# A selective scan and a mixture of experts on one core: the order of TensorE's slot, the last chain, the ring of gate rows and the adder of every fourth state

## The reference, cut to what matters

```python
x = x + mamba_block(ln_c(x))         # x: (4, 128, 16, 16); 4 batches, 128 channels, 256 positions
# inside: four chunks of 32 channels, each: h = dA * h + (dt*x) * B_t for 16 states, 256 steps,
#         y = sum over states of h * C_t; y = (y + xc * D) * silu(z); out projection; layer norm; proj
t = to_tokens(x)
t = t + moe(ln_t(t))                 # 16 experts, hidden 256, top 2 by router logits
#         out = sum over e of ce[e] * ((silu(t @ wg[e]) * (t @ wu[e])) @ wd[e]), all experts computed
```

## Time and profile before

| | us |
|---|---|
| median of 3 runs (lowest, highest) | 334.9 (333.28, 337.46) |
| the profiled execution's own time | 334.86 |
| its span, first to last instruction | 333.1 |
| mean granted TensorE clock, share of full | 0.969 |
| PE busy | 290.8 |
| DVE busy | 238.1 |
| POOL busy | 168.4 |
| ACT busy | 152.4 |

### The profile page before, as it was taken

The page is one execution under the profiler, slowest core; times in us unless marked ns, Lnnn a source line. Parts: engine busy times, 40 slices in busy tenths (PEclk is TensorE's granted clock), DMA queues, the critical chain, the costliest instruction groups (busy, mean ns, idle before and its releaser), DMA issues.

```text
span 333.1 us, 3808 instructions
## 1 busy us (share of the span) xinstructions
PE 290.8 (87%) x1172; PEld 212.2 (64%) x1172; DVE 238.1 (71%) x380; ACT 152.4 (46%) x228; POOL 168.4 (51%) x155
## 2 busy tenths in 40 slices
PE   7986799989699989876699887688899998699996
PEld 5842645545355767654576766466678786588885
DVE  2479899999586976989769769877864364355543
ACT  2578755535453337564333376533423562222221
POOL 5000898886338566877498659765821220322310
PEclk9999769999979999999979999979999999999999
DMA  7991666337822864655748666641110200221110
GB/s 262 349 281 39 201 211 201 126 126 202 191 85 78 200 186 129 186 143 135 212 107 224 173 145 171 157 130 64 47 37 28 63 31 4 63 80 48 48 32 16
DMA packets 21748, 43.39 MB, mean 130 GB/s; under 512 B 2848, under 2 KB 8032, under 8 KB 21728
## 3 DMA queue, kind: packets, MB, share of 16 engines
q1 hardware_dynamic: 16848, 34.09, 36.1%
q10 hardware_dynamic: 4880, 9.07, 9.5%
HBM read 42.03 MB, written 1.11 MB: 130 GB/s over the span
## 4 chain that ended last, share of the span: by engine, by line
PE 44%; issue 28%; POOL 14%; DVE 8%; ACT 4%; DMA 1%; POOLq 0%; DVEq 0%; ACTq 0%
PE bank L730 17%; POOL y L311 7%; PE bank L911 7%; PE bank L878 7%; PE bank L896 7%; POOL u L304 5%; PE bank L734 3%; DVE y L567 2%; POOL xs L318 2%; DMA X<-x 1%; ACT th L500 1%; PE bank L792 1%; ACT bank L438 1%; DVE dt L571 1%; DVE y L576 1%
## 5 line engine op out<-in xcount | busy, mean ns | idle before, releaser
L500 ACT ACTIVATE th<-bank,cst 128x512 f32<-128x512 f32 x64 | 44.0, 687 | 131.6 <-PE bank L878 131.5
L304 POOL TENSOR_TENSOR u<-dtx,BCs 128x512 f32<-128x512 f32 x64 | 81.0, 1276 | 15.3 <-DVE h L624 14.6
L896 PE MATMUL bank<-xs,Wu 128*128 128x256 f32 x256 | 67.9, 388 | 21.6 <-DVE hid L694 15.1
L686 DVE SCALAR_TENSOR_TENSOR th<-th,bank 128x512 f32<-128x512 f32 x64 | 43.9, 686 | 59.4 <-ACT th L500 59.2
L318 POOL TENSOR_TENSOR xs<-xm,Gs 128x512 f32<-128x512 f32 x32 | 41.0, 1283 | 83.5 <-DMA Gs<-CE_far 79.3
L896 PEld LDWEIGHTS bank<-xs,Wu 128*128 128x128 f32 x256 | 47.5, 192 | 37.9 <-issue 20.8
L878 PE MATMUL bank<-xm,Wg 128*128 128x256 f32 x256 | 67.5, 387 | 0.0
L911 PE MATMUL bank<-hid,Wd 128*128 128x256 f32 x256 | 67.0, 386 | 0.0
L438 ACT ACTIVATE bank<-dt,cst,A 128x510 f32<-128x510 f32 x64 | 49.6, 775 | 20.1 <-DVE h L624 17.8
L878 PEld LDWEIGHTS bank<-xm,Wg 128*128 128x128 f32 x256 | 49.8, 195 | 7.5 <-issue 0.5
L911 PEld LDWEIGHTS bank<-hid,Wd 128*128 128x128 f32 x256 | 48.5, 192 | 8.5 <-issue 2.1
(11 more groups left out here) (120 smaller groups left out, 220.1 us busy)
## 6 DMA issues: line engine op xcount, KB each, us to landing
BCs<-BC_far SPq DMA_DIRECT2D x72, 256.0 KB, 4.1
Gs<-CE_far ACTq DMA_DIRECT2D x32, 256.0 KB, 3.4
BCs<-BC_far SPq DMA_DIRECT2D x56, 128.0 KB, 3.1
Wg<-gate_w SPq DMA_DIRECT2D x1, 2048.0 KB, 10.7
Wu<-up_w SPq DMA_DIRECT2D x1, 2048.0 KB, 16.2
par<-params ACTq DMA_DIRECT2D x1, 597.5 KB, 4.4
X<-x SPq DMA_DIRECT2D x2, 256.0 KB, 4.7
BC_far<-BC_rows SPq DMA_DIRECT2D x4, 128.0 KB, 3.0
```

The lines of the kernel that those rows point to most:

```text
L304: g.tensor_tensor(u[:, k % U_RING], dtx[:, k // NS, :], BCs[:, k % BC_RING, 0], ALU.mult)\
L500: a.activation(th[:, n % 2], bank[gate_bank(n)][:], ACT.Tanh, scale=0.5, bias=zero).then_inc(S["th_r"], 1)
L686: v.scalar_tensor_tensor(th[:, n % 2], th[:, n % 2], 1.0, bank[gate_bank(n)][:], ALU.add, ALU.mult)\
L896: o = t.matmul(bank[up_bank(n)][:, f * T:(f + 1) * T], Wu[:, e, f * P:(f + 1) * P], xs[:, pr % 2, ts], start=True, stop=True)
```

## The change

G_RING goes from 3 to 4, and ACT issues each spread one pair of items further ahead (three of them where a batch begins). PE's slot becomes `gate(n+1)`, `up(n)`, chain item, `down(n-2)`, `sum_state`; `gate(0)` goes before the last of the first 28 steps and waits for weighed state 25 of those instead of 26 (bank 2's last reader is step 24). States 3, 7, 11 of the last two batches (k % 4 == 3) are summed by PE instead of POOL, for which the product with D, which starts the bank's sum, moves from offset 11 to 3. The last batch's chain has a table of its own, `BESIDE_TAIL`, in which the later items come 1 to 2 offsets earlier and ACT's "spread" is at offset 9. The warming products go from 8 to 11 at the start and from 16 to 4 before the projections, and end two steps earlier in the steps; the products of the variance go ahead of those that prepare weights.

```diff
--- before.py
+++ after.py
@@ -38,7 +38,7 @@
 LAG = 2
 BY_PE = 2 * NS
 BC_RING = 6
-G_RING = 3
+G_RING = 4
 U_RING = HC_RING = 4
 H_RING = 3
 LAST_C2 = FIRST - 2
@@ -48,9 +48,11 @@
                 "PE": {1: "out", 2: "var", 4: "centre", 5: "var_t", 7: "logits", 8: "turn", 9: "x1"},
                 "ACT": {1: "sq", 2: "rstd", 4: "sq_t", 5: "rstd_t", 7: "exp", 8: "gates", 9: "x1", 10: "spread"}}
 BESIDE_ITEMS = {"DVE": {0: "gated", 3: "norm", 6: "tokens", 7: "top", 8: "mix"},
-                "PE": {0: "total", 1: "out", 2: "var", 4: "centre", 5: "var_t", 7: "logits", 9: "turn", 10: "x1",
-                       11: "skip_D"},
+                "PE": {0: "total", 1: "out", 2: "var", 4: "centre", 5: "var_t", 7: "logits", 9: "turn", 10: "x1", 3: "skip_D"},
                 "ACT": {1: "sq", 2: "rstd", 4: "sq_t", 5: "rstd_t", 8: "exp", 9: "gates", 10: "x1"}}
+BESIDE_TAIL = {"DVE": {0: "gated", 2: "norm", 4: "tokens", 5: "top", 6: "mix"},
+               "PE": {0: "total", 1: "out", 2: "var", 3: "centre", 4: "var_t", 5: "logits", 7: "turn", 8: "x1"},
+               "ACT": {1: "sq", 2: "rstd", 3: "sq_t", 4: "rstd_t", 6: "exp", 7: "gates", 8: "x1", 9: "spread"}}
 
 F32, F32R, U32 = mybir.dt.float32, mybir.dt.float32r, mybir.dt.uint32
 ALU, ACT = mybir.AluOpType, mybir.ActivationFunctionType
@@ -183,7 +185,7 @@
 
 
         def by_pe(k):
-            return k < BY_PE or k % NS == NS - 1
+            return k < BY_PE or k % 4 == 3
 
         def red_count(k):
             return sum(1 for i in range(k) if by_pe(i))
@@ -202,7 +204,7 @@
             b, o = divmod(k, NS)
             if b - 1 not in range(BATCH):
                 return None, None
-            table = (BESIDE_STEPS if b == 1 else BESIDE_ITEMS)[engine]
+            table = (BESIDE_STEPS if b == 1 else BESIDE_TAIL if b == BATCH else BESIDE_ITEMS)[engine]
             return table.get(o), b - 1
 
         block = ctx.enter_context(nc.Block())
@@ -490,8 +492,10 @@
                     act.wait_ge(S["bias_r"], 1)
                     a.activation(X[:, b, :], bank[R][:, T:2 * T], ACT.Identity, bias=bias[:]).then_inc(S["x1_r"], 1)
                 if item == "spread":
-                    spread_gate(0)
-                    spread_gate(1)
+                    spread_gate(b * E // 2)
+                    spread_gate(b * E // 2 + 1)
+                    if b == 0:
+                        spread_gate(2)
 
             def gate_tanh(n):
                 act.wait_ge(S["g_r"], n + 1)
@@ -519,10 +523,11 @@
                 if k + 1 < STEPS:
                     decay(k + 1)
                 back(*chain("ACT", k), True)
-                if n % E == E - 2 and n + 2 < ITEMS:
+                if n % E == E - 2 and n // E < BATCH - 2:
                     spread_gate(n // 2 + 1)
-                pr = n // 2 + 2
-                if n % 2 == 0 and pr < ITEMS // 2 and 2 * pr % E:
+                    spread_gate(n // 2 + 2)
+                pr = n // 2 + 3
+                if n % 2 == 0 and pr < ITEMS // 2 and pr % (E // 2) > 1:
                     spread_gate(pr)
 
         @block.vector
@@ -734,25 +739,25 @@
                     t.matmul(bank[b][:, 0:P], mean_w[:], mean_w[:], start=True, stop=True)
 
             pe.wait_ge(S["mean_c"], 1)
-            keep_warm(8, 6)
+            keep_warm(11, 6)
             pe.wait_ge(S["M_r"], 1)
             for i in range(2):
                 pe.wait_ge(S[f"x_in{i}"], 16)
                 mm(bank[i][:], M[:], half(X, i), "cen_r")
+            pe.wait_ge(S["const0"], 7)
+            for i in range(2):
+                pe.wait_ge(S["sq_r"], i + 1)
+                mm(bank[2 + i][:], var_in_w, half(sq, i), "var_r")
             pe.wait_ge(S["par_in"], 16)
             mm(bank[7][:, 0:P], p("out0"), M[:], "prep_r")
             mm(bank[7][:, P:2 * P], p("out1"), M[:], "prep_r")
             mm(bank[7][:, 2 * P:3 * P], p("dt_in"), p("dt_out"), "prep_r")
             mm(bank[7][:, 3 * P:3 * P + 1], p("proj"), p("norm_b"), "prep_r")
             mm(bank[6][:, 0:P], p("proj_t"), M[:], "prep_r")
-            pe.wait_ge(S["const0"], 7)
-            for i in range(2):
-                pe.wait_ge(S["sq_r"], i + 1)
-                mm(bank[2 + i][:], var_in_w, half(sq, i), "var_r")
             pe.wait_ge(S["bias_r"], 1)
             pe.wait_ge(S["projw_r"], 2)
             mm(bank[6][:, P:P + 1], M[:], bias[:], "bias_p")
-            keep_warm(16, 5)
+            keep_warm(4, 5)
 
             def project_in(i, base, weights, name):
                 for turn, (b, q) in enumerate(((0, 0), (1, 1), (0, 1), (1, 0))):
@@ -852,15 +857,6 @@
                     t.matmul(r2, proj_w[:], chk[:, b, :], start=True, stop=False)
                     mm(r2, ident[:], X[:, b, :], "x1p_r", False, True)
 
-            for k in range(FIRST):
-                back(*chain("PE", k))
-                if k + 1 < FIRST:
-                    spread_c(k + 1)
-                if k:
-                    sum_state(k - 1)
-                if k < FIRST - 2:
-                    keep_warm(1, 7)
-
             def gate(n):
                 b, e = divmod(n, E)
                 if n == 0:
@@ -871,7 +867,7 @@
                 if j:
                     pe.wait_ge(S["m_r"], j)
                 elif n == 0:
-                    pe.wait_ge(S["hc_r"], LAST_C2)
+                    pe.wait_ge(S["hc_r"], LAST_C2 - 1)
                 else:
                     pe.wait_ge(S["scan_r"], FIRST)
                 for f in range(FH):
@@ -912,16 +908,25 @@
                                  start=e == 0 and f == 0, stop=e == E - 1 and f == FH - 1)
                 o.then_inc(S["yd_r"], 1)
 
-            gate(0)
+            for k in range(FIRST):
+                if k == FIRST - 1:
+                    gate(0)
+                back(*chain("PE", k))
+                if k + 1 < FIRST:
+                    spread_c(k + 1)
+                if k:
+                    sum_state(k - 1)
+                if k < FIRST - 4:
+                    keep_warm(1, 7)
             for n in range(ITEMS):
                 k = step_at(n)
+                if n + 1 < ITEMS:
+                    gate(n + 1)
                 up(n)
                 back(*chain("PE", k))
                 if n >= LAG:
                     down(n - LAG)
-                if n + 1 < ITEMS:
-                    gate(n + 1)
-                if k - 1 < BY_PE:
+                if k - 1 < STEPS and by_pe(k - 1) and (k - 1 < BY_PE or k % NS):
                     sum_state(k - 1)
             for n in range(ITEMS - LAG, ITEMS):
                 down(n)
```

## The result

The changed kernel takes 305.35 us (median of 4 runs, 304.15 to 307.34), the kernel before 334.25 us in the same series (4 runs). The ratio is 0.913, with an interval of 0.904 to 0.921. The forecast was 310.0 with a range of 303 to 320. The profiled execution is the slowest of the four, 307.34 us, of which 305.5 are span.

The account below looks back on a forecast made before the run. The prediction took the rounds to be bound by waits, no engine being full, and PE alone to matter after slot 36. 333.1 - 15.0 - 1.2 - 7.1 - 1.2 = 308.6 us of span, forecast 310, range 303 to 320.

Parts of the forecast that it names:

- The slot order: Rounds of slots 5 to 20 and 21 to 36: gate product first would gain 15.0 us, range 7 to 21.
- the ring: Fourth gate-row buffer: counted in the rounds; price outside them 0, from -0.5 to +1 us.
- the states: Six state additions moved from POOL to PE, 5.2 us of PE work: alone a loss of 0 to 5 us.
- Rival D: The middle doesn't move, the gate product being late for another reason: 9.5 us won elsewhere, 325 us; chance 0.05.
- rival F: Slower: gate product stands ahead of an up product DVE already waits for, 0.866 us a slot, 356 us; chance 0.03.
- The replay's 55.1: Round replayed instruction by instruction: floor 51.3 plus 4.0 us losses, 1.0 for a batch's first scaled tokens; 57 taken.
- The last batch's chain: From slot 36: 6.2 us from removing all but 0.4 of 6.6 waiting, plus 0.9; together 7.1 (4 to 8).
- Entry: Gate product 0 one state sum earlier, 0.9 us, and 0.3 over slots 0 to 4: 1.2 (0 to 2).
- Beginning: Warming and variance order before the steps: gain 1.2 us, from a loss of 1 to 2.
- rival E: The clock falls after the shortened warming, projections up to 5 us longer: 315 to 320 us; chance 0.06.
- B: PE becomes the bound of the rounds, 60.5 us each, 8 won instead of 15: 317 us; chance 0.19.
- C: All waits go and the clock stays up, rounds of 54.5, beginning 2: 304 us; chance 0.11.

Follow-up runs that it names:

- tail: The changed kernel with the last batch's chain back at its old offsets and spread, gate product still first: 307.36 us.
- variance: The changed kernel with the products that prepare the weights again ahead of those of the variance: 303.96 us.
- the earlier chain's run: The changed kernel with the end of the chain of batches 1 and 2 one slot earlier, DVE's top and mix together: 302.23 us.
- the best version: The changed kernel with the chain's end one slot earlier, only state 15 of the last two batches on PE, and weights before variance: 299.03 us.

## Why the prediction was right, and where it was not

**The slot order: right in its mechanism, and in its sum.** 15.0 us were forecast for the rounds and 15.4 measured. The loop of late gate product, late tanh and late DVE is what went: its edit alone brings 334 to 304.3 us, and everything else without it brings nothing. The forecast counted the ring and the states into the same term; they add nothing to it. Rival D (the product is late for another reason) and rival F (a gate product in the way of an up product that DVE waits for) have fallen. The wait that F needs is there, 8.9 us in 9 times, but 5.4 of it lie at the two handovers (2.28 + 2.11 + 0.61 + 0.42), and it doesn't stop DVE from being busy 51.2 of 54.9 us.

**The replay's 55.1, and the 57 taken.** The second round took 54.9, so the replay was good to 0.2 us, and the 1.9 us that I added for what a replay doesn't see were not needed there. In the four other profiles with the same code at that place (tail, 8 and 16 warming products, variance) the second round takes 55.0 to 55.3. The first round took 58.7, and its excess is nearly all at one place, the handover, which the replay had at 1.0 us. Its size belongs to the execution: those four have first handovers of 7.9, 8.1, 7.9 and 10.6 us. The two long ones, 10.8 and 10.6, are those in which PE stood 2.6 to 2.8 us and slow products followed; the rounds of the other three take 55.9 to 56.0. The two misses, 1.7 too little and 2.1 too much, happened to cancel: that is luck.

**The ring: right.** Price 0, measured 0.4 us with runs 1 to 3 us apart.

**States for PE: right.** A loss inside 0 to 5 us; 0.75 a round by the trace and 2.2 us by the medians. POOL had nothing to win.

**The last batch's chain: the size was right, the cause wrong.** The step that failed is "the rest, 6.6, is waiting", as far as it gave the waits' end to the new offsets. The working named both ("With the gate product first and the new offsets") and didn't take them apart. By the experiments the order gives 6.5 of 7.4 us. The waits for the combine weights and for the scaled tokens (1.38 and 2.50) came from engines being late in the slots before, by the same late gate product as in the rounds. Once it isn't late, the old offsets cost 0.64 us of waiting.

**Entry: right in the part that can be read, the rest is not the change's for sure.** 1.2 us were forecast, 2.4 measured. The 0.9 for the earlier gate product 0 came true: DVE's wait for the first tanh is 1.85 us in every variant that has it and 2.71 in the two that have not the earlier trace rows, 0.86 less. The 0.3 for slots 0 to 4 was undersized, and it is the slot order's and not gate product 0's: these slots take 12.50 us with an early gate product 0 and the late others, and 11.66 with the order alone. The other 0.8 us are in the steps before the items. They take 63.0 to 64.5 us in variants that differ nowhere in that stage, with a granted clock that dips in slices 5 to 7 by varying amounts; the stage has no finer reading, and the extra 0.8 us are not shown to be the change's.

**Beginning: the number on the table is mostly luck, and one part had the wrong sign.** 1.2 us were forecast and 2.4 measured, but the run with the order alone, whose beginning is that of the kernel before, has its first scan at 35.96 us, 0.15 after the changed kernel's 35.81. Most of the 2.4 is thus a slow beginning in the one profiled execution of the kernel before. The step that failed is the worth of the three edits there. The shorter second warming gives 1.9 us (307.21 against 305.28). The longer first one gives nothing, where 1.4 was thought possible if the clock rose. The variance ahead of the weights costs 1.3 us where I said "no gain": I had looked at DVE's norm behind the weights' end and not at DVE's own copy, which then comes between variance and norm. Together they are worth some 0.6 us, half of what was forecast. The difference of centring, 3.75 against 2.27, belongs to the executions: with 16 records of warming it took 3.75 once and 1.96 twice.

**The clock after shorter warming (rival E): fallen.** The projections run at the same 0.16 us a record as before (32 records in 5.17 us), and the granted clock of the first 35.8 us is 0.95, before 0.96. The rule that I had weighed, in the Trainium skill, TensorE: Matmul & The Clock Gate, Part 1, says that the array starts throttled and that activity lifts it. Each beginning here agrees with it in kind: a record of warming takes 0.24 us at the start (16 in 3.79) and 0.12 in the second warming (32 in 3.82). What I took from it does not tell which of two executions with the same 16 records is fast at 5.5 us; no run here shows what does.

**Rivals B and C.** The first round, 58.7, came near B's 60.5, though not for B's reason; the second round and the tail are C's. The measured 305.35 lies between C's 304 and A's 310. Had I kept the replay's 55.1, the sum would have come to 310.4 - 3.8 = 306.6 us.

## What to carry to other kernels

Where engines work in fixed orders on a ring of work, put first in a slot the product whose inputs are long ready and which has the longest way to its user, and last what nobody waits for. Replay a round before and after: it was good to 0.2 us here for an undisturbed round. Measure such a package edit by edit: one move in this one was worth 30 us, two others (states on PE, the variance first) cost 1 to 2 us each, and the tail's new offsets, a gain of 0.9 beside the early gate product, go with a loss of 4 beside the late one. And before a difference at the beginning is put down to an edit, look at a second execution of the same code.

## What was not expected of the hardware

- The time at which TensorE's first products become fast varies from execution to execution with the same code ahead of it: four records of centring at 5.5 to 5.8 us took 1.88 to 2.52 us in thirteen profiles and 3.75 in one. The 3.75 and two of the 1.96 had the same 16 records of warming ahead of them, the others 22. The row of the granted clock doesn't show it: it reads 1.00 over the first 12 us of the slow beginning too.
- How long PE stood doesn't by itself tell whether slow products follow. The wait of 2.84 us was followed by products at 1.77 and 1.92 us instead of 1.03, one of 2.76 us by 1.54 and 1.91, and the one of 2.14 in the earlier chain's run by 1.53 and 1.91. But one of 2.70 us with the late gate product, 2.50 at item 48 before and 2.11 with the ring of 3 were followed by none that were slow, and one of 1.39 us in the best version, before the product with the combine weights at 192.50 us, by 1.91 and 1.60. At item 16 it made the wait of 2.84 us dearer by some 1.7 (0.10, 0.74 and 0.89 over the usual 1.03 each).
- A 256 KB spread of one row of gates at a batch's beginning took 3.1 to 6.6 us from issue to POOL's product where POOL stood for it, with 5.4 and 3.8 in the same profile of the changed kernel. There PE asks for the tokens of items 16 and 32 at 3.9 us after the issue (155.70 - 2.84 - 148.95, and 212.28 - 1.17 - 207.19), and POOL's 1.3 us lie in that too, so both come late.
